# Grouped square roots, three score banks on each side and single-bank score units in a streamed attention kernel

## The chip, the cores and the metric

The kernel runs on one core of a Trainium2 chip. The metric is the device time of one execution in microseconds (us). TensorE (PE) multiplies matrices into PSUM, which has eight banks of 128 x 512 f32; VectorE (DVE), ScalarE (ACT) and GpSimd (POOL) work elementwise; SyncE (SP) issues most DMAs. Each engine runs its own instructions in order and waits for the others by semaphores.

## The reference

The input x is 8 sequences of 512 tokens of 128 channels, in f32. Eight layers follow, each x = x + f(layernorm(x)):

```python
x = x + L0_attn_a(ln(x))   # causal attention, 16 heads of 8 channels
x = x + L0_ffn(ln(x))      # sqrt((x @ cos A)^2 + (x @ sin A)^2)
x = x + L0_attn_b(ln(x))   # full attention with RoPE, 16 heads of 8
x = x + L0_ffn(ln(x))
x = x + L1_attn_a(ln(x))   # linear attention, then a GELU MLP inside
x = x + L1_ffn(ln(x))      # fp4-quantised gated MLP
x = x + L1_attn_b(ln(x))   # one head: softmax over the query axis of q k^T / 128
x = x + L1_ffn(ln(x))
```

The modulus in L0_ffn is the square root that the change groups.

## The kernel before, in words

The residual x stays in SBUF for the whole kernel as the tile X, four tiles of 128 tokens for each sequence. The six programs run one after the other with a barrier between: STREAM (`attention_stream`), linear attention, GELU MLP, fp4 MLP, `query_softmax`, fp4 MLP.

**The stream** computes the first four lines of the reference. It has 16 items (n = 0 to 15): items 0 to 7 are the eight sequences in layer a (causal), items 8 to 15 the same sequences in layer b (full). The heads of an item are worked on in four quads of four heads. `stream_order` writes down a time, in quads, for every piece of work; the list is sorted by it, and each engine walks the list in that order and does its own share. Nothing is reordered while it runs. For one quad:

- "first": the first score pass. PE writes q k^T, queries on partitions, into one of two PSUM banks (FIRST, L589). DVE takes the row maximum, with the mask added in layer a (L752), without in layer b (L757). The maxima are negated, turned (L597), copied by ACT (L476) and sent by DMA into the stacked queries.
- "scores": the second pass, two quads later (LAG). PE writes the scores, keys on partitions and the maximum already subtracted (L613), into one of two pairs of banks (SECOND). ACT takes the exponential of a unit into one of four `probs` tiles of 128 x 1024 (L500). A unit is two heads of 512 queries in layer b (8 units a quad); in layer a it is two heads or four, with the masked part left out (6 units a quad). In layer a POOL clears the half of the diagonal block that lies in the future (L380).
- "sum": PE multiplies the values with `probs` for one tile of keys, four heads side by side (L630), when the last unit of these keys is ready. ACT copies the sums (L508), PE turns them (L540), DVE divides.

PSUM is thus split as FIRST 0-1, SECOND 2-5, SUMS 6, MISC 7. MISC is used by turns for projections (L566, L570, L575), transposes, the turned maxima and the L0_ffn products.

After the last quad of an item comes its L0_ffn: layer norm, two products with cos and sin (L661), squares on ACT (L527), their sum on POOL (L391, `m_sum`), the square root on ACT (L531, `lengths`), the addition to x on POOL (L399, `m_add`). The square root needs another activation table than the exponential, so a table load stands before L531 and one before the next L500. There is one such square root for each item. The scratch of this part (m_xn, m_total and others) lies in X1, which the stream does not use otherwise.

**`query_softmax`** is a software pipeline over eight sequences with four stages, MEASURE, PROJECT, SCORE and SUM. `run_steps` emits steps with all engines' share; with four stages steps 4 to 7 form a hardware loop of two passes. In each step DVE does, in this order: normalise for PROJECT (L845), statistics for MEASURE, row maxima for SCORE (L1414), the value bias (L1421), the scaling of values (L1428), and the addition of SUM's result to X (L1433).

Of the kernel before, what the change touches and what calls it, by code (L numbers as in the profile page):

```python
# [84 lines left out]
LAG = 2  # L85


def score_units(causal):

    if not causal:  # L90
        first = [(qt, (j,), 512, 512) for qt in range(4) for j in range(4)]
        second = [(kt, pair, 512, 512) for kt in range(4) for pair in ((0, 1), (2, 3))]
        return first, second
    first = [(0, (0, 1, 2, 3), 128, 128), (1, (0, 1), 256, 256), (1, (2, 3), 256, 256)]
    first += [(qt, (j,), (qt + 1) * 128, 512) for qt in (2, 3) for j in range(4)]
    second = [(kt, pair, (4 - kt) * 128, 512) for kt in (0, 1) for pair in ((0, 1), (2, 3))]
    second += [(2, (0, 1, 2, 3), 256, 256), (3, (0, 1, 2, 3), 128, 128)]
    return first, second


def stream_order(seqs, late_loads):
# [9 lines left out]
    for n in range(2 * seqs):  # L111
        if n < seqs:
            f_at = [u / 11 for u in range(11)]
            s_at = [0.04, 0.20, 0.36, 0.50, 0.66, 0.82]
            sum_at = [0.50, 0.78, 1.03, 1.17]
            copy_at, tail_at = 1.19, 1.50
        else:
            f_at = [u / 16 for u in range(16)]
            s_at = [(i + 0.20) / 8 for i in range(8)]
            sum_at = [(kt + 1.45) / 4 for kt in range(4)]  # L120
            copy_at, tail_at = 1.20, 1.44
# [51 lines left out]
        at(r + 2.25, "mroot", n)  # L173
        at(r + 2.65, "madd", n)
# [5 lines left out]
def attention_stream(core, seqs, w, layers):  # L180
# [6 lines left out]
    def layer(n):  # L187
        return n // seqs
# [35 lines left out]
    probs = [sb(f"probs{i}", [P, 1024]) for i in range(4)]  # L224
# [10 lines left out]
    m_xn, m_total = spare[:, 0:4], spare[:, 4:8]  # L235
    m_xT = spare[:, 8:12].rearrange("p a c -> p (a c)")
    m_squares = [spare[:, 12 + 4 * i:16 + 4 * i].rearrange("p a c -> p (a c)").rearrange("p (t c) -> p t c", t=2)
                 for i in range(2)]
    angle, turns = [spare[:, 20 + 2 * i:22 + 2 * i].rearrange("p a c -> p (a c)") for i in range(2)]
# [7 lines left out]
    FIRST, SECOND, SUMS, MISC = 0, 2, 6, 7  # L247
# [78 lines left out]
    def gpsimd(g):  # L326
# [46 lines left out]
        def clear_future(n, q, gq, i):  # L373
            if not causal[layer(n)]:
                return
            _, heads, width, stride = second_of(n)[i]
            u = seconds(gq) + i
            diagonal = probs[u % 4][:].rearrange("p (h c) -> p h c", c=stride)[:, 0:len(heads), 0:P]
# [8 lines left out]
        def m_sum(n, q, gq, i):  # L387

            g.wait_ge(misc_free, uses_of_misc("mpart", n, 0, 1))
            for half in range(2):  # L390
                last = g.tensor_tensor(m_total[:, 2 * half:2 * half + 2], m_squares[half][:, :, 0:P],  # L391
                                       m_squares[half][:, :, P:2 * P], ALU.add)
            last.then_inc(m_total_ready, 1)

        def m_add(n, q, gq, i):
            b = n % seqs
            xs = X[:, 4 * b:4 * b + 4, :]
            g.wait_ge(m_length_ready, n + 1)
            g.tensor_tensor(xs, xs, m_total, ALU.add).then_inc(m_added, 1)  # L399
# [41 lines left out]
    def scalar(act):  # L441
# [48 lines left out]
        def exponentials(n, q, gq, i):  # L490

            _, heads, width, stride = second_of(n)[i]
            u = seconds(gq) + i
            b = u % 2
            src = ps[:, SECOND + 2 * b:SECOND + 2 * b + 2, :].rearrange("p a c -> p (a c)")
            v = lambda t: t.rearrange("p (h c) -> p h c", c=stride)[:, 0:len(heads), 0:width]
            act.wait_ge(scores_ready, u + 1)
            if u >= 4:
                act.wait_ge(sums_ready, freed_by(u - 4))
            act.activation(v(probs[u % 4][:]), v(src), ACT.Exp, scale=layers[layer(n)]["scale"])\  # L500
                .then_inc(scores_free, 1)
# [35 lines left out]
    def tensor(pe):  # L537
# [40 lines left out]
        def first_scores(n, q, gq, u):  # L578

            qt, heads, width, stride = first_of(n)[u]  # L580
            U = firsts(gq) + u
            if q % 2 == 0 and u == 0:

                pe.wait_ge(stack_loaded[q // 2], 16 * STACK_DMAS * (n + 1))
            if U >= 2:
                pe.wait_ge(max_free, U - 1)
            for o, j in enumerate(heads):
                h = 4 * q + j
                last = pe.matmul(ps[:, FIRST + U % 2, o * stride:o * stride + width],  # L589
                                 QS[n % 2][0:SHIFT_AT, h, qt * P:(qt + 1) * P], KS[n % 2][0:SHIFT_AT, h, 0:width],  # L590
                                 start=True, stop=True)
            last.then_inc(max_ready, 1)
# [7 lines left out]
        def scores(n, q, gq, i):  # L600
# [7 lines left out]
            if u >= 2:  # L608
                pe.wait_ge(scores_free, u - 1)
            for o, j in enumerate(heads):  # L610
                h = 4 * q + j
                bank, c = SECOND + 2 * (u % 2) + o * stride // 512, o * stride % 512
                last = pe.matmul(ps[:, bank, c:c + width], KS[n % 2][:, h, kt * P:(kt + 1) * P],  # L613
                                 QS[n % 2][:, h, 512 - width:512], start=True, stop=True)
            last.then_inc(scores_ready, 1)

        def sum_keys(n, q, gq, kt):
# [8 lines left out]
            for u, (at, heads, width, stride) in enumerate(second_of(n)):  # L626
                if at != kt:
                    continue
                for o, j in enumerate(heads):
                    last = pe.matmul(ps[32 * j:32 * j + DH + 1, SUMS, 512 - width:512], V[n % 2][:, kt, 4 * q + j, :],  # L630
                                     probs[(seconds(gq) + u) % 4][:, o * stride:o * stride + width],
# [37 lines left out]
    def vector(v):  # L669
# [71 lines left out]
        def maxima(n, q, gq, u):  # L741
            qt, heads, width, stride = first_of(n)[u]
            U = firsts(gq) + u
            src = ps[:, FIRST + U % 2, :].rearrange("p (h c) -> p h c", c=stride)[:, 0:len(heads), 0:width]
# [558 lines left out]
def query_softmax(core, items, w):  # L1303
# [25 lines left out]
    MEASURE, PROJECT, SCORE, SUM = range(4)  # L1329

    def gpsimd(g):
        def step(s, par, on):
            if on(MEASURE):
                root(g, s, par)
        run_steps(g, items, 4, step, before=1)


    def scalar(act):
# [19 lines left out]
        run_steps(act, items, 4, step, before=1)  # L1358

    def tensor(pe):  # L1360
# [37 lines left out]
        run_steps(pe, items, 4, step, before=1)  # L1398

    def vector(v):  # L1400
        v.sem_inc(out_free, 2)

        def step(s, par, on):
            if on(PROJECT):
                n, p = s - PROJECT, (par - PROJECT) % 2
                wait(v, misc_full, 4 * (n - 1) + 1)
                apply(v, n, xn[p], tiles(X, n, per), p).then_inc(xn_ready, 1)
            if on(MEASURE):
                measure(v, tiles(X, s, per), par)
# [24 lines left out]
        run_steps(v, items, 4, step, before=1)  # L1434
# [611 lines left out]
```

## Time and profile before

| | us |
|---|---|
| runs of the kernel | 2019.5, 2023.92 (median), 2027.14 |
| the profiled execution, its own time | 2022.12 |
| its span in the trace | 2020.4 |
| of that the stream | about 993 |
| of that `query_softmax` | 1755 to 1872 |

| engine | busy us (share of the span) |
|---|---|
| PE | 1686.0 (83%) |
| DVE | 1410.2 (70%) |
| ACT | 1056.4 (52%) |
| POOL | 520.4 (26%) |

The granted TensorE clock is a share of full speed. A busy PE is not a PE at its peak: the ends of matmuls are modelled, and the end of one overlaps the next.

### The profile page before, as it was taken

The numbers are of one execution on the slowest core, as the hardware profiler recorded it, in microseconds if no ns is written. First come the engines' busy times: TensorE is split into PE (matmuls) and PEld (weight loads), VectorE is DVE, ScalarE is ACT, GpSimd is POOL, SyncE is SP. The second block draws the span as 40 slices with busy tenths as digits, with TensorE's granted clock in tenths as the row PEclk, the third lists the DMA queues.
The fourth block names the chain that finished last, engine by engine and source line by source line (L and its number), as shares of the span: only waits on it lengthen the run. The fifth ranks groups of instructions, "written<-read, shape, count | busy, mean of one in ns | idle before, by whom it ended". The sixth has DMA issues, their size and how long they took to land. (4 is left out here: it accounts for less than half of the span.)

```text
span 2020.4 us, 36743 instructions
## 1 busy us (share of the span) xinstructions
PE 1686.0 (83%) x12704; PEld 941.8 (47%) x12781; DVE 1410.2 (70%) x4005; ACT 1056.4 (52%) x1727; POOL 520.4 (26%) x579
## 2 busy tenths in 40 slices
PE   3788888888988989888699999999997866688566
PEld 1233333333333333232366767767675645445454
DVE  6677777788777877775266667766674588655787
ACT  1466666656666666666354544445442355333453
POOL 5455555553333223300100000000002422200222
PEclk9799999999999999999699999999998988789798
DMA  5434332222221122200000000000000000000000
GB/s 95 58 62 96 61 65 49 49 47 46 48 48 24 25 48 48 40 9 1 0 1 2 2 2 2 2 3 1 2 2 1 1 0 0 1 0 0 6 16 21
DMA packets 56691, 49.82 MB, mean 25 GB/s; under 512 B 9221, under 2 KB 54469, under 8 KB 56517
## 3 DMA queue, kind: packets, MB, share of 16 engines
q1 hardware_dynamic: 53692, 46.45, 12.2%
q10 hardware_dynamic: 2824, 1.11, 0.4%
q8 instruction: 102, 1.67, 0.4%
q14 instruction: 73, 0.59, 0.1%
HBM read 7.10 MB, written 2.10 MB: 5 GB/s over the span
## 5 line engine op out<-in xcount | busy, mean ns | idle before, releaser
L500 ACT ACTIVATE at_probs<-ps 128x1024 f32<-128x1024 f32 (+1 forms) x448 | 427.6, 962 | 279.7 <-PE ps L613 273.7
L757 DVE TENSOR_REDUCE at_M<-ps 128x1 f32<-128x512 f32 x512 | 336.7, 686 | 109.5 <-PE ps L589 108.7
L589 PE MATMUL ps<-at_KS,at_QS 96*128 96x512 bf16 (+3 forms) x1024 | 321.8, 352 | 53.5 <-DVE at_M L752 21.0
L752 DVE CUSTOM_DVE_ANT_0 at_masked<-ps,at_mask_row 128x384 bf16<-128x384 f32 (+3 forms) x512 | 228.9, 486 | 74.9 <-PE ps L589 72.8
L630 PE MATMUL ps<-at_probs,at_V 128*9 128x512 f32 (+3 forms) x2048 | 233.0, 527 | 27.1 <-ACT at_C L508 12.3
L613 PE MATMUL ps<-at_QS,at_KS 128*128 128x512 bf16 x947 | 242.9, 343 | 15.1 <-DMA at_QS<-at_nmT 7.5
L589 PEld LDWEIGHTS ps<-at_KS,at_QS 96*128 96x128 bf16 x1024 | 91.6, 98 | 334.6 <-DVE at_M L757 150.7
L380 POOL TENSOR_SCALAR_AFFINE_SELECT at_probs<-at_probs 128x256 f32<-128x256 f32 (+1 forms) x192 | 93.9, 492 | 179.8 <-ACT at_probs L500 178.9
L613 PEld LDWEIGHTS ps<-at_QS,at_KS 128*128 128x128 bf16 x1024 | 93.2, 99 | 83.1 <-issue 25.2
L839 POOL TENSOR_TENSOR la_rstd<-la_vare,mhalf 128x4 f32<-128x4 f32 x16 | 16.1, 1008 | 414.7 <-DVE la_vare L834 414.7
L1250 DVE SCALAR_TENSOR_TENSOR la_phiq<-ps,la_ezq 128x512 f32<-128x512 f32 x64 | 44.2, 690 | 111.8 <-ACT la_ezq L1101 111.8
L1579 POOL TENSOR_TENSOR fp_rounded<-fp_level,fp_scale 128x960 f32<-128x960 f32 (+2 forms) x36 | 59.1, 1641 | 188.8 <-DVE fp_level L1734 188.8
L1678 PE MATMUL ps<-gate_up,fp_xT 128*128 128x352 f32 x256 | 104.0, 559 | 2.5 <-ACT fp_xT L1602 2.5
L1195 PE MATMUL ps<-la_V,la_S 128*64 128x65 f32 x2048 | 103.0, 221 | 0.2 <-issue 0.2
L1259 DVE TENSOR_TENSOR la_S<-ps,keep_kq 128x512 f32<-128x512 f32 x128 | 82.4, 685 | 27.0 <-PE ps L1167 26.1
L1088 ACT ACTIVATE la_V<-ps 128x512 f32<-128x512 f32 x64 | 38.2, 597 | 111.3 <-PE ps L1141 111.3
L1095 ACT ACTIVATE la_belowq<-ps 128x512 f32<-128x512 f32 x64 | 38.2, 597 | 110.8 <-PE ps L1148 110.8
L1660 PE MATMUL ps<-ident,fp_rounded 128*128 128x128 f32 x64 | 15.0, 319 | 92.8 <-POOL fp_rounded L1579 92.8
L1195 PEld LDWEIGHTS ps<-la_V,la_S 128*64 128x64 f32 x2048 | 91.7, 137 | 0.4 <-issue 0.4
L630 PEld LDWEIGHTS ps<-at_probs,at_V 128*9 128x9 f32 x2048 | 31.1, 88 | 103.8 <-issue 40.8
L1191 PE MATMUL ps<-la_state,la_phiq 128*64 128x130 f32 x768 | 75.5, 275 | 0.0
L1678 PEld LDWEIGHTS ps<-gate_up,fp_xT 128*128 128x128 f32 x256 | 57.3, 235 | 36.8 <-issue 18.0
(258 smaller groups left out, 3373.7 us busy)
## 6 DMA issues: line engine op xcount, KB each, us to landing
at_QS<-at_splitq SPq DMA_DIRECT2D x288, 64.0 KB
at_KS<-at_splitk SPq DMA_DIRECT2D x279, 64.0 KB
out<-X SPq DMA_DIRECT2D x8, 256.0 KB, 2.3
at_QS<-at_nmT ACTq DMA_DIRECT2D x64, 8.0 KB
at_KS<-at_splitk ACTq DMA_DIRECT2D x9, 64.0 KB
w_raw<-fp_weights SPq DMA_DIRECT2D x1, 560.0 KB, 5.7
w_wv<-L_attn_a_wv SPq DMA_DIRECT2D x1, 512.0 KB, 6.8
w_wo<-L_attn_a_wo SPq DMA_DIRECT2D x1, 512.0 KB, 6.6
```

The costliest lines, as they stand in the source:

```text
L380: g.affine_select(out=diagonal, in_=diagonal, compare_op=ALU.is_ge, fill=0.0, base=0, pattern=[[0, len(heads)], [1, P]], channel_multiplie ...
L500: act.activation(v(probs[u % 4][:]), v(src), ACT.Exp, scale=layers[layer(n)]["scale"])\
L589: last = pe.matmul(ps[:, FIRST + U % 2, o * stride:o * stride + width], QS[n % 2][0:SHIFT_AT, h, qt * P:(qt + 1) * P], KS[n % 2][0:SHIFT_A ...
L613: last = pe.matmul(ps[:, bank, c:c + width], KS[n % 2][:, h, kt * P:(kt + 1) * P], QS[n % 2][:, h, 512 - width:512], start=True, stop=True)
L630: last = pe.matmul(ps[32 * j:32 * j + DH + 1, SUMS, 512 - width:512], V[n % 2][:, kt, 4 * q + j, :], probs[(seconds(gq) + u) % 4][:, o * s ...
L752: last = v.tensor_tensor_reduce(masked[U % 4][:, o * stride:o * stride + width], src[:, o, :], mask_row[:, 512 - width:512], 1.0, 4 * NEG, ...
L757: v.tensor_reduce(M[gq % 2][:, heads[0]:heads[-1] + 1, qt], src, AX.X, ALU.max).then_inc(max_free, 1)
L1191: pe.matmul(outs[rows, c, 0:2 * AUG], phi[0][j % 4][:, c * P:(c + 1) * P][:, rows], state[j % 2][:, c - 1, :], start=True, stop=False)
L1195: last = pe.matmul(outs[rows, c, AUG * a:AUG * (a + 1)], S[a][j % 2][:, c * P:(c + 1) * P][:, rows], V[par][:, c, 2 * j + a, :], start=c = ...
L1259: v.tensor_tensor(S[a][j % 2][:].rearrange("p (c q) -> p c q", c=4), ps[:, SCORES + a, :].rearrange("p (c q) -> p c q", c=4), over(core["k ...
L1579: g.tensor_tensor(in_blocks(rounded[par][:, lo:hi]), in_blocks(level[par][:, lo:hi]), over(scale[par][:, lo // BLOCK:hi // BLOCK], 2, BLOC ...
L1678: last = pe.matmul(ps[:, GATE_UP + 2 * t + i, 0:INNER], xT[p][:, t * P:(t + 1) * P], gate_up[:, i, :], start=True, stop=True)
```

## The change

- A second-pass unit is now at most 512 columns, one bank: one head in layer b (16 units a quad), one head, two of 256 or four of 128 in layer a (11 units a quad). The times of the units in the order are new; those of the sums are not.
- FIRST and SECOND have three banks each. The waits for a free bank look back three units instead of two. `probs` becomes eight tiles of 128 x 512, the same space.
- The square root waits until up to four items have their sums of squares: items 0-3, 4-7, 8-11, 12-14 and 15. m_total has four parts; one `activation` covers those of a group, and the additions to x follow 0.4 quads apart.
- In `query_softmax` the addition to X becomes a fifth stage, ADD, one step later, between the normalising and the statistics. With five stages `run_steps` emits no hardware loop for eight items: all steps are written out.

```diff
+ROOTS = 4
+def root_group(n, items):
+    first = n - n % ROOTS
+    last = min(first + ROOTS, items) - 1
+    if last == items - 1:
+        return (n, n) if n == last else (first, last - 1)
+    return first, last
...
-        second = [(kt, pair, 512, 512) for kt in range(4) for pair in ((0, 1), (2, 3))]
+        second = [(kt, (j,), 512, 512) for kt in range(4) for j in range(4)]
...
-    second = [(kt, pair, (4 - kt) * 128, 512) for kt in (0, 1) for pair in ((0, 1), (2, 3))]
-    second += [(2, (0, 1, 2, 3), 256, 256), (3, (0, 1, 2, 3), 128, 128)]
+    second = [(kt, (j,), (4 - kt) * 128, 512) for kt in (0, 1) for j in range(4)]
+    second += [(2, (0, 1), 256, 256), (2, (2, 3), 256, 256), (3, (0, 1, 2, 3), 128, 128)]
...
-            s_at = [0.04, 0.20, 0.36, 0.50, 0.66, 0.82]
+            s_at = [0.03, 0.11, 0.19, 0.27, 0.35, 0.43, 0.50, 0.57, 0.66, 0.74, 0.83]
...
-            s_at = [(i + 0.20) / 8 for i in range(8)]
+            s_at = [(i + 0.20) / 16 for i in range(16)]
...
-        at(r + 2.25, "mroot", n)
-        at(r + 2.65, "madd", n)
+        lo, hi = root_group(n, 2 * seqs)
+        if n == hi:
+            at(r + 2.25, "mroot", n)
+            for i in range(hi - lo + 1):
+                at(r + 2.65 + 0.4 * i, "madd", lo + i)
...
-    probs = [sb(f"probs{i}", [P, 1024]) for i in range(4)]
+    probs = [sb(f"probs{i}", [P, 512]) for i in range(8)]
...
-    FIRST, SECOND, SUMS, MISC = 0, 2, 6, 7
+    FIRST, SECOND, SUMS, MISC = 0, 3, 6, 7
...
-            act.wait_ge(m_total_ready, n + 1)
-            act.activation(m_total, m_total, ACT.Sqrt).then_inc(m_length_ready, 1)
+            lo, hi = root_group(n, items)
+            act.wait_ge(m_total_ready, hi + 1)
+            some = spare[:, 16 + 4 * (lo % ROOTS):20 + 4 * (hi % ROOTS)]
+            act.activation(some, some, ACT.Sqrt).then_inc(m_length_ready, hi - lo + 1)
...
-            if U >= 2:
-                pe.wait_ge(max_free, U - 1)
+            if U >= 3:
+                pe.wait_ge(max_free, U - 2)
...
-            if u >= 2:
-                pe.wait_ge(scores_free, u - 1)
+            if u >= 3:
+                pe.wait_ge(scores_free, u - 2)
...
-    MEASURE, PROJECT, SCORE, SUM = range(4)
+    MEASURE, PROJECT, SCORE, SUM, ADD = range(5)
...
+            if on(ADD):
+                n, p = s - ADD, (par - ADD) % 2
+                xs = tiles(X, n, per)
+                v.wait_ge(out_ready, n + 1)
+                v.tensor_tensor(flat(xs), flat(xs), ps[:, OUT + p, :], ALU.add).then_inc(out_free, 1)
             if on(MEASURE):
...
-            if on(SUM):
-                n, p = s - SUM, (par - SUM) % 2
-                xs = tiles(X, n, per)
-                v.wait_ge(out_ready, n + 1)
-                v.tensor_tensor(flat(xs), flat(xs), ps[:, OUT + p, :], ALU.add).then_inc(out_free, 1)
```

## Rows read from the trace of the kernel before

**Rows 1.** Busy time by engine in the stretches of layers a, b and `query_softmax`.

```profile
core 0: us, PE busy (x) PEld busy (x) DVE busy (x) ACT busy (x) POOL busy (x), PEclk, DMA share, GB/s
90.00:435.00 345.00, 292.00 (x2179) 134.31 (x2206) 266.11 (x1189) 215.40 (x299) 189.05 (x269) 0.98 0.33 63
435.00:945.00 510.00, 455.94 (x2474) 160.43 (x2521) 387.33 (x832) 334.42 (x404) 144.74 (x141) 0.98 0.18 34
...
1755.00:1872.00 117.00, 93.80 (x448) 61.21 (x448) 63.11 (x200) 39.04 (x89) 8.06 (x8) 0.89 0.00 1
```

**Rows 2.** The same for one sequence of layer b, quad by quad.

```profile
690.52:709.01 18.49, 15.35 (x82) 5.39 (x81) 13.16 (x25) 13.57 (x17) 10.66 (x11) 1.00 0.04 10
709.01:724.29 15.28, 14.50 (x69) 4.16 (x71) 9.88 (x19) 9.28 (x12) 6.79 (x6) 0.89 0.49 84
724.29:739.80 15.51, 14.74 (x89) 5.98 (x88) 11.95 (x25) 9.91 (x14) 0.00 (x0) 1.00 0.29 61
739.80:755.07 15.27, 13.68 (x75) 4.87 (x77) 13.84 (x40) 9.70 (x14) 2.03 (x2) 1.00 0.01 2
```

**Rows 3.** Waits in total: who waited for whom, us, times, longest us.

```profile
ACT at_probs L500 <- PE ps L613: 273.7, 308, 8.5
...
PEld ps L589 <- DVE at_M L757: 150.7, 262, 1.1
...
PEld ps L589 <- DVE at_M L752: 72.0, 127, 1.3
...
PEld ps L630 <- ACT at_probs L500: 36.1, 68, 4.2
...
PEld ps L570 <- ACT at_nmT L476: 26.3, 14, 2.3
...
PEld ps L630 <- POOL at_probs L380: 22.7, 38, 2.6
```

**Rows 4.** Order of time, ACT and PE around a square root of layer b.

```profile
702.17 1.93 ACT L500 ACTIVATE at_probs<-ps 128x1024 f32<-128x1024 f32 x2
...
704.70 1.28 ACT L531 ACT_TABLE_LOAD   x1
...
706.64 1.28 ACT L500 ACT_TABLE_LOAD   x1
...
708.86 0.25 ACT L476 ACTIVATE at_nmT<-ps 32x128 bf16<-32x128 bf16 x1
...
709.16 1.19 PE L570 MATMUL ps<-at_xT,w_b_wk 128*128 128x512 f32 x2 [2.02 <-ACT at_nmT L476]
```

**Rows 5.** Groups by shape in the first 1200 us: busy us, mean ns | idle before.

```profile
L500 ACT ACTIVATE at_probs<-ps 128x1024 f32<-128x1024 f32 x352 | 359.1, 1023 | 224.3 <-PE ps L613 218.3 <-remote 3.2
...
L380 POOL TENSOR_SCALAR_AFFINE_SELECT at_probs<-at_probs 128x256 f32<-128x256 f32 x128 | 52.3, 412 | 117.5 <-ACT at_probs L500 116.7
...
L380 POOL TENSOR_SCALAR_AFFINE_SELECT at_probs<-at_probs 128x512 f32<-128x512 f32 x64 | 41.7, 651 | 62.4 <-ACT at_probs L500 62.2
...
L500 ACT ACTIVATE at_probs<-ps 128x512 f32<-128x512 f32 x32 | 19.1, 597 | 39.3 <-PE ps L613 39.3
...
L531 ACT ACTIVATE X<-X 128x512 f32<-128x512 f32 x16 | 10.1, 629 | 0.4 <-POOL X L391 0.2
```

**Rows 6.** Order of time, PE at a first-pass matmul of layer b.

```profile
744.98 0.60 PE L613 MATMUL ps<-at_QS,at_KS 128*128 128x512 bf16 x2
745.56 0.39 PE L589 MATMUL ps<-at_KS,at_QS 96*128 96x512 bf16 x1
746.41 0.39 PE L589 MATMUL ps<-at_KS,at_QS 96*128 96x512 bf16 x1 [0.46 <-DVE at_M L757]
```

**Rows 7.** Order of time, DVE and PE between two steps of `query_softmax`.

```profile
1806.29 0.69 DVE L1428 TENSOR_TENSOR qs_vs<-qs_val,qs_inverse 128x512 f32<-128x512 f32 x1
1807.43 0.69 DVE L1433 TENSOR_TENSOR X<-X,ps 128x512 f32 x1 [0.45 <-PE ps L1395]
1808.04 1.11 DVE L845 TENSOR_SCALAR qs_xn<-X,qs_meanvar,qs_rstd 128x128 f32 x4
...
1809.28 0.65 PE L1367 MATMUL ps<-ident,qs_xn 128*128 128x128 f32 x4 [2.03 <-DVE qs_xn L845]
```

More of the change, by code:

```diff
@@ L234, in attention_stream @@
     spare = core["X1"]
-    m_xn, m_total = spare[:, 0:4], spare[:, 4:8]
-    m_xT = spare[:, 8:12].rearrange("p a c -> p (a c)")
-    m_squares = [spare[:, 12 + 4 * i:16 + 4 * i].rearrange("p a c -> p (a c)").rearrange("p (t c) -> p t c", t=2)
+    m_xn = spare[:, 0:4]
+    m_xT = spare[:, 4:8].rearrange("p a c -> p (a c)")
+    m_squares = [spare[:, 8 + 4 * i:12 + 4 * i].rearrange("p a c -> p (a c)").rearrange("p (t c) -> p t c", t=2)
                  for i in range(2)]
-    angle, turns = [spare[:, 20 + 2 * i:22 + 2 * i].rearrange("p a c -> p (a c)") for i in range(2)]
+    m_total = [spare[:, 16 + 4 * i:20 + 4 * i] for i in range(ROOTS)]
+    angle, turns = [spare[:, 28 + 2 * i:30 + 2 * i].rearrange("p a c -> p (a c)") for i in range(2)]
     m_stats = sb("m_stats", [P, 4, 6])
@@ L389, in m_sum @@
             g.wait_ge(misc_free, uses_of_misc("mpart", n, 0, 1))
+            if n == ROOTS - 1:
+                g.wait_ge(waves_ready, 1)
             for half in range(2):
-                last = g.tensor_tensor(m_total[:, 2 * half:2 * half + 2], m_squares[half][:, :, 0:P],
+                last = g.tensor_tensor(m_total[n % ROOTS][:, 2 * half:2 * half + 2], m_squares[half][:, :, 0:P],
                                        m_squares[half][:, :, P:2 * P], ALU.add)
@@ L493, in exponentials @@
             u = seconds(gq) + i
-            b = u % 2
-            src = ps[:, SECOND + 2 * b:SECOND + 2 * b + 2, :].rearrange("p a c -> p (a c)")
+            src = ps[:, SECOND + u % 3, :]
             v = lambda t: t.rearrange("p (h c) -> p h c", c=stride)[:, 0:len(heads), 0:width]
             act.wait_ge(scores_ready, u + 1)
-            if u >= 4:
-                act.wait_ge(sums_ready, freed_by(u - 4))
-            act.activation(v(probs[u % 4][:]), v(src), ACT.Exp, scale=layers[layer(n)]["scale"])\
+            if u >= 8:
+                act.wait_ge(sums_ready, freed_by(u - 8))
+            act.activation(v(probs[u % 8][:]), v(src), ACT.Exp, scale=layers[layer(n)]["scale"])\
                 .then_inc(scores_free, 1)
@@ L607, in scores @@
                     pe.wait_ge(signs_loaded, 16 * 2)
-            if u >= 2:
-                pe.wait_ge(scores_free, u - 1)
+            if u >= 3:
+                pe.wait_ge(scores_free, u - 2)
             for o, j in enumerate(heads):
                 h = 4 * q + j
-                bank, c = SECOND + 2 * (u % 2) + o * stride // 512, o * stride % 512
-                last = pe.matmul(ps[:, bank, c:c + width], KS[n % 2][:, h, kt * P:(kt + 1) * P],
+                c = o * stride
+                last = pe.matmul(ps[:, SECOND + u % 3, c:c + width], KS[n % 2][:, h, kt * P:(kt + 1) * P],
                                  QS[n % 2][:, h, 512 - width:512], start=True, stop=True)
@@ L1334, in step @@
                 root(g, s, par)
-        run_steps(g, items, 4, step, before=1)
+        run_steps(g, items, 5, step, before=1)
     def scalar(act):
@@ L1357, in step @@
                                    scale=SCALE, accum_out=total[p][:, t:t + 1]).then_inc(E_ready, 1)
-        run_steps(act, items, 4, step, before=1)
+        run_steps(act, items, 5, step, before=1)
     def tensor(pe):
@@ L1397, in step @@
                 last.then_inc(out_ready, 1)
-        run_steps(pe, items, 4, step, before=1)
+        run_steps(pe, items, 5, step, before=1)
     def vector(v):
@@ L1428, in step @@
                 v.tensor_tensor(vs[p][:], val[p][:], over(inverse[p][:], 2, P), ALU.mult).then_inc(vs_ready, 1)
-            if on(SUM):
-                n, p = s - SUM, (par - SUM) % 2
-                xs = tiles(X, n, per)
-                v.wait_ge(out_ready, n + 1)
-                v.tensor_tensor(flat(xs), flat(xs), ps[:, OUT + p, :], ALU.add).then_inc(out_free, 1)
-        run_steps(v, items, 4, step, before=1)
+        run_steps(v, items, 5, step, before=1)
     return dict(gpsimd=gpsimd, scalar=scalar, tensor=tensor, vector=vector)
```

12 lines of the change are left out of this document (6 added, 6 removed).

## The prediction, made before the changed kernel was run

> **What bounds the kernel now.** I first read busy time by stretch. In the stream no engine is full: PE is busy 292 of 345 us in layer a and 456 of 510 in layer b, DVE 266 and 387, ACT 215 and 334 [rows 1]. The PE figure is flattered. In [rows 6] a first-pass matmul starts 0.58 us after a pair that needs 0.43 (two at about 0.215, the pace at which such matmuls follow each other: the pair's 0.60 us is two paces plus a tail of 0.17), and the next one 0.85 us later, so 0.63 us is empty where the row books 0.46. So I take it that PE, DVE and ACT hold each other up: each walks a fixed order, and a late engine stops the others because only two banks lie between them.
>
> Then one sequence of layer b, quad by quad [rows 2]. It takes 64.55 us. The quads look alike but for the first, 18.49 us against 15.3 to 15.5, and the second has a granted clock of 0.89, which is 0.11 x 15.28 = 1.7 us lost at half speed. The last quad has DVE busy 13.84 of 15.27 us: there DVE is nearly the bound. In the second it is busy only 9.88.
>
> The waits say what stops PE [rows 3]. The weight loads of the first pass waited for DVE for 150.7 + 72.0 = 222.7 us over 389 times, 0.57 us each. The k projection waited for ACT's copy of the turned maxima for 26.3 us, 14 times in 16 items, 1.88 us each. Sums waited for ACT 36.1 us and for POOL's mask 22.7 us. ACT waited for PE 273.7 us: as a whole it has room. The order of time around a square root [rows 4] explains the k projection: ACT loads a table at 704.70, takes the root, loads the other table at 706.64, goes on with exponentials at 707.92, and reaches the copy at 708.86, for which PE has stood 2.02 us at L570.
>
> **Square roots.** Each costs ACT 1.28 + 0.63 + 1.28 = 3.2 us in one piece [rows 4, 5]. Of 16 single ones, 11 go (items 0-2, 4-6, 8-10, 12, 13). What a block costs in time is not 3.2 us but what PE waits behind it: 1.88 us on average, 2.02 in the row shown, and in some cases part of the 1.7 us of low clock that follows the wait. I take 2.2 us: 11 x 2.2 = 24 us gained. The blocks kept grow: per 512 elements an exponential costs 1023 - 597 = 426 ns more [rows 5], so a root over four items takes 3 x 0.43 = 1.3 us more and over three 0.85. Three of four, one of three: 3 x 1.3 + 0.85 = 4.7 us, fully on the path since PE waits there already; I take 4. Net -20. Bounds: +5 (ACT is late anyway) and -45 (all 3.2 us and some clock). What is late next is the k projection's own chain, copy of the maxima, which then waits for an exponential or two only. The additions on POOL keep their number, 16; four now follow a root 0.4 quads, some 6 us, apart. No DMA is added or moved, and SP's waits for stacks look at the same events. The last item keeps its own root, so the end of the stream is as before.
>
> The Trainium skill (ScalarE: Activation LUTs, "What ACT_TABLE_LOAD costs") puts a switch at 2.66 us, load and drain together. The trace shows 1.28 us from load to next work, so the measurement decides; by the page 22 fewer switches would be 58 us of ACT, by the row 28.
>
> **Three banks for the first pass.** The most that can be won is the true emptiness behind the 389 waits. Of the mean 0.57 us a part is still filled by the pair streaming since the last load: 0.43 less one load of 0.10 is 0.33, so 0.24 us is empty, 389 x 0.24 = 93 us. A third bank lets PE be one more maximum, some 0.62 us of DVE work, ahead. It helps where DVE was held by something passing (the wait for a layer norm's root, a block of four small operations), and not where DVE is full, as in the last quad of [rows 2]. I take a little over a third: -35. Bounds 0 and -93.
>
> **Single-bank units.** Exponentials: layer a 6 to 11 a quad, layer b 8 to 16, over 32 quads each: 448 become 864, 416 more. Two in a row of 1024 take 1.93 us where each lasts 1.02 [rows 4], so 0.11 us of an operation hides under the next one. If ACT is always supplied, an extra instruction costs (0.597 - 0.11) x 2 - (1.023 - 0.11) = 0.06 us, if each is met alone 2 x 0.597 - 1.023 = 0.17 us: 25 to 71 us more of ACT. It has 273.7 us of waits for PE to put them in, so mostly nothing. What is lost is elasticity: PE may lead ACT by two units of 0.91 us before and by three of 0.49 us now, 1.8 against 1.5 us, and the sums stand closer behind their last unit (in layer b 0.16 quads after it instead of 0.21, 2.5 us instead of 3.2). POOL's masks: 6 selects become 11. By 412 and 651 ns for 256 and 512 columns [rows 5] one of 128 is about 0.29 us, so a quad has 8 x 0.29 + 2 x 0.41 + 0.65 = 3.8 us instead of 4 x 0.41 + 2 x 0.65 = 2.9; POOL is busy 189 of 345 us in layer a [rows 1], with operations of up to 1.28 us in which a mask is queued, and sums behind it. Against this a unit is free sooner for PE. I take +12 us for the whole. Bounds -5 and +71.
>
> The Trainium skill (same page and section) gives an ACTIVATE a fixed 186 ns beside 0.833 ns an element, 93 ns of which hide under the one before. This speaks against the split. By it the 416 cost at least 39 us of ACT, an estimate between the two ends above; the rows agree in the slope (426 ns for 512).
>
> **`query_softmax`.** Between two steps [rows 7] DVE ends the scaling at 1806.98, waits for PE's sum, adds from 1807.43, and normalises only from 1808.04; PE starts the next transposes at 1809.28 after an idle 2.03 us. With the addition behind the normalising, the latter can start at about 1807.0, 1.0 us earlier, and then DVE's chain over ACT's last exponential sets the pace. The addition then delays the statistics and with them the first row maximum, by about 0.5 us, but the exponentials wait for the projection copies on ACT, later than the maxima. Five such steps have a normalising after an addition: -5. Written-out steps I put at nothing: the loop's seam shows no gap to remove. A higher clock (0.89 here [rows 1]) adds perhaps 1: -6 in all. Bounds -2 and -12.
>
> **Sum.** 2022.1 - 20 - 35 + 12 - 6 = 1973 us, on the profiled execution's own time. The median of the runs is 1.8 us above that: 1975 us.
>
> **Rivals.**
>
> - DVE is the bound and a third bank changes nothing. For it: DVE busy 13.84 of 15.27 us in one quad. Against: 9.9 to 13.2 in the other three. 2022 - 20 + 12 - 6 = 2008. Chance 0.22.
> - The three engines come apart well. Roots -30, first pass -60, units +5, `query_softmax` -9: 1928. For it: even with the tails counted PE books 58.3 of the 64.55 us of [rows 2], so without waits a sequence of layer b could shrink by 6 us and more, eight of them by 50. Against: half of what is empty is at other waits (MISC, sums). Chance 0.20.
> - ACT's splitting lands on the path: slower. If the exponentials are met one at a time and each quad's sums wait for them, all 71 us count: 2022 - 20 - 35 + 71 - 6 = 2032; it needs 61 of the 71 us on PE's path to decide against the kernel, and with the first-pass gain gone, 26. For it: sums already waited 36.1 us for ACT. Against: 273.7 us of room. Chance 0.10, of which 0.07 ends above 2034.
> - Masks late: in layer a POOL's extra 0.9 us a quad all in front of sums, +29 instead of a few: 1995. It lies in the forecast's neighbourhood and is counted there.
>
> The forecast (1950 to 2000) has 0.48.
>
> **Numbers.** The range is 1930 to 2016: it leaves out the upper part of the third rival and part of the second. A measurement can tell about 0.5%, 10 us. Faster than 2014: 0.84; within: 0.09; slower than 2034: 0.07. Within the likeliest case alone 1950 to 2000.
>
> **What would show it.** The 18.5 us quads of layer b become about 16 except after grouped roots, with waits of L570 for the copy near 0 in 11 items; two table loads per group, 10 in place of 32. The waits of L589 for DVE fall by a third or more. Exponentials of 512 last 0.60 us each and ACT's busy time changes by the 25 to 71 us above less some 30 for loads and roots. Sums' waits for POOL and ACT rise somewhat. Transposes L1367 wait about 1 us in place of 2. The prediction is wrong if PE's waits only change their names: second-pass matmuls waiting for ACT, or DVE at over 90% in all quads.

## The result and the profile after

The changed kernel takes 1952.63 us in the median of four runs (1949.83 to 1954.47), against 2022.47 before: 0.9651 of it, 95% interval [0.9628, 0.9675], 70 us less. (2022.47 is the median of four runs of the kernel before; the 2023.92 above was that of three.) The range given, 1930 to 2016, held it; the forecast was 1975. The profiled execution took 1949.83 us.

The page of the changed kernel, its span and the busy time by engine:

```profile
span 1948.0 us, 37580 instructions
...
PE 1659.1 (85%) x12701; PEld 945.7 (49%) x12781; DVE 1400.6 (72%) x4005; ACT 1046.9 (54%) x2110; POOL 543.9 (28%) x739
```

PE's work is the same, yet it books 27 us less. Part of that is the clock: the mean granted clock of the stream rises from 0.96 to 0.97, and the share missing to full speed times the time is 40 us before and 28 now, some 12 us less (an estimate from rounded rows). The rest may lie in the modelled ends of matmuls, which overlap more where matmuls follow each other closely; that isn't shown. The barrier behind the stream falls at about 930 us instead of 993, 63 of the 72 us by which the spans differ; `query_softmax` gives 11.7, and the other programs together take about 2 us more.

Busy time by engine of the changed kernel, quad by quad in one sequence of layer b without a root, then the stretch of `query_softmax` from its first transposes to its last sum, in the kernel before and in the changed one; columns as in [rows 1] and [rows 2] (the stretch in [rows 1] is a wider one):

```profile
592.20:608.00 15.80, 14.49 (x79) 5.34 (x80) 11.40 (x24) 10.63 (x23) 8.31 (x9) 1.00 0.01 2
608.00:620.86 12.86, 12.80 (x72) 4.14 (x71) 10.64 (x21) 9.66 (x21) 7.91 (x7) 1.00 0.48 80
620.86:635.59 14.73, 14.17 (x89) 6.12 (x89) 11.71 (x25) 10.07 (x21) 0.00 (x0) 1.00 0.43 93
635.59:649.99 14.40, 13.54 (x77) 4.91 (x78) 14.04 (x41) 10.28 (x21) 2.03 (x2) 1.00 0.00 1
```

```profile
1759.06:1871.23 112.17, 93.80 (x448) 61.17 (x448) 59.74 (x186) 39.04 (x89) 7.05 (x7) 0.90 0.00 1
```

```profile
1697.60:1798.10 100.50, 88.32 (x448) 59.14 (x448) 58.24 (x187) 39.00 (x89) 7.05 (x7) 0.94 0.00 1
```

Against [rows 2] the sequence takes 57.79 us instead of 64.55. The first quad falls from 18.49 to 15.80, the second from 15.28 to 12.86 and shows the full clock, 1.00 for 0.89. In the last quad DVE is busy 14.04 of 14.40 us, so it is close to being the bound there. What each part of the change gave in these quads stands with the experiments.

Waits of the changed kernel in total, those of [rows 3] (L606 is the first pass, L630 the second, L647 the sums, L587 the k projection):

```profile
ACT at_probs L515 <- PE ps L630: 162.8, 221, 5.1
...
PEld ps L606 <- DVE at_M L774: 105.8, 174, 0.9
...
PEld ps L647 <- ACT at_probs L515: 56.1, 109, 1.5
...
PEld ps L606 <- DVE at_M L769: 50.9, 81, 1.1
...
PEld ps L647 <- POOL at_probs L394: 38.4, 66, 3.9
...
PEld ps L630 <- ACT at_probs L515: 30.6, 48, 4.1
...
PEld ps L587 <- ACT at_nmT L492: 11.6, 11, 5.5
```

The first pass waits for DVE 255 times and 156.7 us instead of 389 and 222.7. The sums wait more, 94.5 us for 58.8. The second pass waits for ACT (30.6 us; before it was 5.0). The k projection waits 11.6 us for 26.3, but its longest wait has grown from 2.3 to 5.5 us: that is a grouped root.

Timeline of the changed kernel around a grouped root in layer b on ACT (start, duration, and then the work):

```profile
721.68 1.28 ACT L548 ACT_TABLE_LOAD   x1
722.97 1.91 ACT L548 ACTIVATE X<-X 128x2048 f32<-128x2048 f32 x1
724.90 1.28 ACT L515 ACT_TABLE_LOAD   x1
...
727.17 0.25 ACT L492 ACTIVATE at_nmT<-ps 32x128 bf16<-32x128 bf16 x1
```

The same stretch on PE, then PE behind the grouped root of layer a; in brackets the wait and what ended it:

```profile
726.85 0.61 PE L630 MATMUL ps<-at_QS,at_KS 128*128 128x512 bf16 x1 [3.04 <-ACT at_probs L515]
...
727.68 1.92 PE L587 MATMUL ps<-at_xT,w_b_wk 128*128 128x512 f32 x2
```

```profile
283.80 2.07 PE L587 MATMUL ps<-at_xT,w_a_wk 128*128 128x512 f32 x2 [5.05 <-ACT at_nmT L492]
```

The block is 4.5 us, as forecast (1.28 + 1.91 + 1.28). In layer b PE first stands at the second pass, where it may lead ACT by three units only. In layer a the copy of the maxima starts 1.5 us after the block has ended (283.49 for 282.03), behind exponentials and the copy of the sums, and PE stands 5.05 us. Both times the projection behind it runs at a low clock: the granted clock is 0.50, the lower level, during the 1.92 us in layer b, and 0.54 in the 6 us from 283.80 on in layer a. In [rows 4] the same pair took 1.19 us.

**One measure for all stream kernels.** ACT copies the sums once a quad, so the distance from one copy (at_C, L508 before, L523 in the changed kernel) to the fourth after it is the time of a sequence. Sequences of the same kind mostly agree within 0.3 us in one kernel, so this resolves what whole runs can't. The exception in the table is units_alone in layer a, from 51.6 to 52.6. The last two columns are the first sequence, and the fourteen behind it taken together.

| us per sequence | a, no root | a, root | b, no root | b, root | the first | the next fourteen |
|---|---|---|---|---|---|---|
| before | | 49.7 | | 64.6 | 46.3 | 807.2 |
| only_roots (grouped) | 45.5 | 55.1 | 60.8 | 67.0 | 43.8 | 779.2 |
| units_alone (single roots) | | 51.6 to 52.6 | | 64.9 | 44.3 | 829.0 |
| first_two_banks (grouped) | 46.7 | 55.4 | 61.5 | 66.4 | 49.6 | 787.5 |
| first_two_second_four (grouped) | 46.7 | 55.3 | 61.5 | 66.3 | 46.6 | 786.4 |
| single_roots | | 50.9 | | 61.4 | 48.1 | 796.2 |
| changed kernel (grouped) | 45.3 | 55.0 | 57.8 | 62.5 | 42.5 | 750.1 |

The first sequence is not a matter of the edits alone: old_qs and qs_written_out below have the changed kernel's stream to the letter, and theirs takes 47.8 and 41.4 us where the changed kernel's takes 42.5. Their next fourteen take 752.0 and 752.2 us. So some 6 us of a difference between whole runs can be an accident of the start.

### The profile page after: what moved, and what is told of

Its sections match the earlier page's. It is cut to its first block and busy times, and to the rows that moved or that the text cites. A ratio compares the mean times of both kernels' runs of the same rounds, so it can differ in the third digit from the quotient of the medians.

```text
span 1948.0 us, 37580 instructions
## 1 busy us (share of the span) xinstructions
PE 1659.1 (85%) x12701; PEld 945.7 (49%) x12781; DVE 1400.6 (72%) x4005; ACT 1046.9 (54%) x2110; POOL 543.9 (28%) x739
## 5 line engine op out<-in xcount | busy, mean ns | idle before, releaser
L515 ACT ACTIVATE at_probs<-ps 128x512 f32<-128x512 f32 (+1 forms) x864 | 458.7, 581 | 219.7 <-PE ps L630 162.8
L774 DVE TENSOR_REDUCE at_M<-ps 128x1 f32<-128x512 f32 x512 | 330.1, 682 | 78.7 <-PE ps L606 77.5
L606 PE MATMUL ps<-at_KS,at_QS 96*128 96x512 bf16 (+3 forms) x1024 | 324.2, 348 | 39.9 <-DMA at_KS<-at_splitk 18.2
L630 PE MATMUL ps<-at_QS,at_KS 128*128 128x512 bf16 x944 | 294.0, 342 | 10.7 <-ACT at_probs L515 10.5
L647 PE MATMUL ps<-at_probs,at_V 128*9 128x512 f32 (+3 forms) x2048 | 228.7, 519 | 26.2 <-POOL at_probs L394 19.2
L606 PEld LDWEIGHTS ps<-at_KS,at_QS 96*128 96x128 bf16 x1024 | 94.4, 99 | 253.0 <-DVE at_M L774 105.8
L394 POOL TENSOR_SCALAR_AFFINE_SELECT at_probs<-at_probs 128x128 f32<-128x128 f32 (+2 forms) x352 | 118.1, 346 | 125.2 <-ACT at_probs L515 119.7
L630 PEld LDWEIGHTS ps<-at_QS,at_KS 128*128 128x128 bf16 x1024 | 97.7, 99 | 101.9 <-ACT at_probs L515 30.6
L647 PEld LDWEIGHTS ps<-at_probs,at_V 128*9 128x9 f32 x2048 | 30.4, 88 | 115.1 <-ACT at_probs L515 56.1
```

The costliest lines, as they stand in the source:

```text
L515: act.activation(v(probs[u % 8][:]), v(src), ACT.Exp, scale=layers[layer(n)]["scale"])\
L606: last = pe.matmul(ps[:, FIRST + U % 3, o * stride:o * stride + width], QS[n % 2][0:SHIFT_AT, h, qt * P:(qt + 1) * P], KS[n % 2][0:SHIFT_A ...
L630: last = pe.matmul(ps[:, SECOND + u % 3, c:c + width], KS[n % 2][:, h, kt * P:(kt + 1) * P], QS[n % 2][:, h, 512 - width:512], start=True, ...
L774: v.tensor_reduce(M[gq % 2][:, heads[0]:heads[-1] + 1, qt], src, AX.X, ALU.max).then_inc(max_free, 1)
```

## The experiments

**The roots: single_roots and only_roots.** The first is the changed kernel with

```diff
-ROOTS = 4
+ROOTS = 1
```

the second the kernel before with `root_group`, four parts of m_total and the grouped `lengths`, and nothing else.

> The changed kernel with one square root for each item again (16 roots instead of 5). By the prediction's price (2.2 us for each root that goes, 4 us back for the longer ones) it takes 20 us more than the changed kernel, 1973 us. Rival: with the new banks PE still leads ACT by only 1.5 us, so a block of 3.2 us on ACT lands on PE's path nearly whole; then 11 x 3.2 less 4.7 is 30 us more and with the clock after each wait up to 38: 1983 to 1991 us. In the trace the first case has PE idle about 2 us at each root, the second 3 us or more.

> The kernel before with the grouped roots alone. By the prediction 20 us less than before, 2002 us; by the rival (the block counts whole) 30 to 38 less, 1984 to 1992. If the root's worth is the same here and in the changed kernel, the parts add up; if it is smaller here, the old two banks hid part of it.

Measured: single_roots 1997.07 us, 0.9877 of before [0.9861, 0.9894], 44 us above the changed kernel. only_roots 1987.86 us, 0.9837 [0.9821, 0.9854], 33 us below before. The price of 2.2 us for a root falls. The table gives its true size: a single root costs 4.2 us (a) and 3.8 (b) in the kernel before (49.7 - 45.5, 64.6 - 60.8), and 5.6 and 3.6 in the changed one. A grouped one costs 4.7 in layer b (62.5 - 57.8) and 9.7 in layer a (55.0 - 45.3). The block is not hidden, and in layer a more than the block is lost. Part of the 9.7 belongs to the place: the one grouped root of layer a falls into the fifth sequence, and with single roots that sequence takes 52.1 us where its neighbours take 50.9 to 51.2. Like for like the grouped root costs 2.9 us more than the single one (55.0 - 52.1), of which 1.3 is its length.

The trace of single_roots shows what comes on top of the block. Its k projection behind a root of layer a, its sequence in layer a, and the same sequence of the changed kernel; then the first two quads of its sequence in layer b:

```profile
201.56 2.08 PE L587 MATMUL ps<-at_xT,w_a_wk 128*128 128x512 f32 x2 [3.78 <-ACT at_nmT L492]
```

```profile
184.93:235.83 50.90, 42.41 (x315) 20.10 (x316) 37.54 (x170) 32.33 (x64) 29.71 (x58) 0.93 0.40 97
```

```profile
174.41:219.75 45.34, 40.09 (x315) 19.20 (x316) 37.45 (x170) 29.01 (x61) 28.49 (x57) 1.00 0.48 109
```

```profile
629.34:647.60 18.26, 15.19 (x81) 5.37 (x81) 12.43 (x25) 13.80 (x25) 10.69 (x11) 0.99 0.04 11
647.60:661.54 13.94, 13.88 (x70) 4.27 (x70) 9.72 (x19) 9.67 (x20) 6.75 (x6) 0.89 0.47 77
```

In layer a PE stands 3.78 us at the k projection, which then runs at a granted clock of 0.50, and the sequence has 0.93 where the changed kernel has 1.00. In layer b the root takes 2.5 us in the first quad (18.26 for 15.80) and 1.1 in the second (13.94 for 12.86), the one with the clock of 0.89.

**The third bank of the first pass: first_two_banks.**

```diff
-            if U >= 3:
-                pe.wait_ge(max_free, U - 2)
+            if U >= 2:
+                pe.wait_ge(max_free, U - 1)
...
-                last = pe.matmul(ps[:, FIRST + U % 3, o * stride:o * stride + width],
+                last = pe.matmul(ps[:, FIRST + U % 2, o * stride:o * stride + width],
```

and the same bank number in `maxima`.

> The changed kernel with two banks for the first pass (the third lies idle). By the prediction the third bank is worth 35 us: 1988 us. Rival: it is worth nothing, DVE being the bound, and the gain in the stream came from the single-bank units: 1952 to 1957 us. A worth between 15 and 50 goes with the prediction.

Measured: 1993.75 us, 0.9868 [0.9851, 0.9884], 41 us above the changed kernel. A sequence without a root is 1.4 us longer in layer a and 3.7 in layer b. The fourteen sequences behind the first are 37 us longer, so most of the 41 is the bank, but 7 us of the distance between the two profiled executions lie in the first sequence, which can be an accident. The waits of its weight loads are somewhat above those of before, 248.3 us for 222.7:

```profile
PEld ps L606 <- DVE at_M L774: 168.2, 280, 1.4
...
PEld ps L606 <- DVE at_M L769: 80.1, 142, 1.1
```

The third bank is what shortened them. Where it helped is told by the quads of a sequence of layer b with two banks, to be set beside those of the changed kernel above:

```profile
619.06:635.31 16.25, 14.81 (x79) 5.16 (x80) 11.37 (x23) 10.83 (x22) 8.31 (x9) 1.00 0.01 2
635.31:649.32 14.01, 13.60 (x72) 3.72 (x71) 10.71 (x21) 10.01 (x20) 7.92 (x7) 1.00 0.42 89
649.32:665.01 15.69, 15.06 (x89) 5.75 (x89) 11.82 (x25) 10.41 (x21) 0.00 (x0) 1.00 0.30 73
665.01:680.59 15.58, 14.18 (x77) 4.50 (x78) 14.32 (x41) 10.58 (x21) 2.02 (x2) 1.00 0.00 1
```

The bank gives 0.45, 1.15, 0.96 and 1.18 us in the four quads. The most comes in the last one, where DVE was busy 14.32 of 15.58 us and the prediction expected nothing.

**A fourth bank for the second pass: first_two_second_four.**

```diff
-    FIRST, SECOND, SUMS, MISC = 0, 3, 6, 7
+    FIRST, SECOND, SUMS, MISC = 0, 2, 6, 7
...
-            if u >= 3:
-                pe.wait_ge(scores_free, u - 2)
+            if u >= 4:
+                pe.wait_ge(scores_free, u - 3)
```

with two first-pass banks, as above.

> The changed kernel with its third first-pass bank given to the second pass: two first, four second. The run with two and three took 1994 us. If PE's short lead over ACT (three units) is what the split costs, a fourth unit gives back 10 to 25 us: 1969 to 1984, though not the 1953 of the changed kernel. Rival: the second pass has banks enough and only the number of operations costs: 1990 to 1996 us.

Measured: 1991.43 us, 0.9858 [0.9818, 0.9898]; first_two_banks had 1993.75. The sequences without a root are the same to 0.1 us, those with one to 0.5. The second pass waits less for ACT, 17.3 us for 27.3, and it gains no time. The rival holds: with two first-pass banks a lead of four units instead of three is worth nothing. So the shorter lead of PE over ACT, which the prediction named as a loss of the single-bank units, shows no cost here.

**The units by themselves: units_alone.** The changed kernel with all three edits undone: `ROOTS = 1`, two first-pass banks, the old `query_softmax`.

> The changed kernel with two banks for the first pass, single roots and the old query_softmax: what is left of the change is the single-bank units, three of them, the eight probs tiles and the new times. The prediction put them at +12 us over before, bounds -5 and +71, which gives 2034 us. If the parts measured so far add up (44 for the roots, 41 for the third first-pass bank, 13 for query_softmax, 98 in sum, where the whole is 70), the units cost 28: 2050 us. If the roots' price depends on the other parts, the result lies nearer to 2030.

Measured: 2042.11 us, 1.0101 of before [1.0063, 1.0139]: longer by 13 to 28 us, 21 in the middle. Its sequences of layer b are 0.3 us longer than before, those of layer a 1.9 to 2.9. In sequences without a root (first_two_banks against only_roots) the units cost 0.7 us in layer b and 1.2 in layer a. There are 256 more exponentials in layer b and 160 in layer a, and layer b loses less. So the longer list of ACT's operations is hardly the main cost; no run tests it by itself.

**The masks: masks_paired.** In layer a one POOL operation clears two neighbouring one-head units; `probs` is one tensor of eight parts for it.

```diff
+            if len(heads) == 1 and i % 2 == 0:
+                return
...
+            if len(heads) == 1 and u % 8:
+                blocks = [(all_probs[:, u % 8 - 1:u % 8 + 1, 0:P], 2, 2)]
```

> The changed kernel with the masks of two neighbouring one-head units of layer a in one POOL operation (7 or 8 a quad instead of 11). The units alone had made a sequence of layer a 2.5 us longer (52.2 against 49.7) and one of layer b only 0.3 (64.9 against 64.6). If that comes from POOL's extra masks, a sequence of layer a shrinks by 1 to 2.5 us: 1934 to 1946 us in all. Rival: it comes from ACT's shorter operations and the sums' shorter distance: 1950 to 1956 us, and layer a stays at 45.3.

Measured: 1949.43 us, 0.9669 [0.9642, 0.9697], not to be told from the changed kernel's 0.9651. POOL's masks fall from 352 to 208 operations:

```profile
L394 POOL TENSOR_SCALAR_AFFINE_SELECT at_probs<-at_probs 128x128 f32<-128x128 f32 x256 | 72.5, 294 | 94.0 <-ACT at_probs L515 90.7 <-DVE at_xn L719 0.9
```

```profile
L404 POOL TENSOR_SCALAR_AFFINE_SELECT at_probs<-at_probs 128x256 f32<-128x256 f32 x176 | 71.7, 409 | 93.0 <-ACT at_probs L525 89.6
```

The first row is of the changed kernel, the second of this one; 128 columns take 294 ns, the 0.29 us estimated. A sequence of layer a stays at 45.2 to 45.6 us: that the number of masks is what the units cost there is not borne out. The test isn't a pure one, since the first unit of a pair now waits for the mask until the second is ready.

**Later sums: sums_later.**

```diff
-            sum_at = [0.50, 0.78, 1.03, 1.17]
+            sum_at = [0.57, 0.85, 1.10, 1.18]
...
-            sum_at = [(kt + 1.45) / 4 for kt in range(4)]
+            sum_at = [(kt + 1.65) / 4 for kt in range(4)]
```

> The changed kernel with each sum as far behind its last unit as before the change (layer b 0.21 quads instead of 0.16, layer a 0.30 instead of 0.23). If the prediction's loss of elasticity lies at the sums, their waits for ACT and POOL (94 us of weight-load waits) fall by half and the time by 5 to 15 us: 1938 to 1948 us. Rival: the sums only pass on how late ACT is, and PE then waits at the next second-pass unit: 1950 to 1956 us.

Measured: 1947.24 us, 0.9620 [0.9582, 0.9659]: by whole runs at the edge of what can be told. By sequences it is plain: 56.6 us instead of 57.8 in layer b, 45.7 to 45.8 instead of 45.3 to 45.4 in layer a. In layer b the shorter distance of the sums cost 1.2 us a sequence, more than the 0.7 that the units cost there; in layer a it cost nothing. The rival was half right: the sums' waits fall from 94.5 to 53.0 us, those of the second pass for ACT rise from 30.6 to 52.6 and those of the first pass for DVE from 156.7 to 171.5, yet time is won. The last quad of a sequence of layer b shows that DVE was not yet its bound in the changed kernel, since it now takes 14.02 us instead of 14.40:

```profile
640.30:654.32 14.02, 13.65 (x77) 4.90 (x78) 13.45 (x40) 10.13 (x21) 2.02 (x2) 1.00 0.00 1
```

**query_softmax: old_qs and qs_written_out.** The first has the old function whole. The second has five stages, and so no hardware loop, but the addition at the end of the step:

```diff
-            if on(ADD):
-                n, p = s - ADD, (par - ADD) % 2
+            if on(SUM):
+                n, p = s - SUM, (par - SUM) % 2
```

moved behind the scaling of the values.

> The changed kernel with query_softmax as it was before (addition at the end of the step, four stages, hardware loop). The prediction had 6 us for it: 1959 us. The two traces differ by 11.7 us from the stage's first transposes to its last matmul (112.2 and 100.5 us), of which the clock is a part; by that the run takes 1964 us, and its stage shows 112 us again.

> The changed kernel with the addition of query_softmax back at the end of the step, but still five stages without a hardware loop. If all of the 12 to 13 us come from the place of the addition, the stage takes 112 us and the run 1965, as with the old one. If the loop itself cost something, it lies between 1953 and 1965.

Measured: old_qs 1965.70 us, 0.9725 [0.9709, 0.9741], 13 above the changed kernel; qs_written_out 1959.28, 0.9687 [0.9651, 0.9723], about half way. The stage in the two, by engine as above:

```profile
1708.80:1820.20 111.40, 93.01 (x448) 61.43 (x448) 59.76 (x186) 39.04 (x89) 7.05 (x7) 0.90 0.00 1
```

```profile
1703.00:1808.60 105.60, 88.16 (x448) 59.20 (x448) 59.36 (x186) 39.00 (x89) 7.05 (x7) 0.94 0.00 1
```

The starts of PE's transposes show why. First with the loop (old_qs), then written out (qs_written_out), then the changed kernel, three steps each:

```profile
1744.21 0.96 PE L1384 MATMUL ps<-ident,qs_xn 128*128 128x128 f32 x4 [1.88 <-DVE qs_xn L862]
1758.40 0.66 PE L1384 MATMUL ps<-ident,qs_xn 128*128 128x128 f32 x4 [2.03 <-DVE qs_xn L862]
1771.00 0.65 PE L1384 MATMUL ps<-ident,qs_xn 128*128 128x128 f32 x4 [2.14 <-DVE qs_xn L862]
```

```profile
1738.38 0.66 PE L1384 MATMUL ps<-ident,qs_xn 128*128 128x128 f32 x4 [1.81 <-DVE qs_xn L862]
1750.71 0.66 PE L1384 MATMUL ps<-ident,qs_xn 128*128 128x128 f32 x4 [1.81 <-DVE qs_xn L862]
1763.04 0.66 PE L1384 MATMUL ps<-ident,qs_xn 128*128 128x128 f32 x4 [1.81 <-DVE qs_xn L862]
```

```profile
1731.84 0.66 PE L1384 MATMUL ps<-ident,qs_xn 128*128 128x128 f32 x4 [0.75 <-DVE qs_xn L862]
1743.11 0.66 PE L1384 MATMUL ps<-ident,qs_xn 128*128 128x128 f32 x4 [0.75 <-DVE qs_xn L862]
1754.38 0.66 PE L1384 MATMUL ps<-ident,qs_xn 128*128 128x128 f32 x4 [0.74 <-DVE qs_xn L862]
```

With the loop a step takes 14.19, then 12.60 us; written out 12.33 and 12.33; with the addition moved 11.27 and 11.27. The four steps of old_qs from 1744.21 on, with their granted clock:

```profile
1744.21:1758.40 14.19, 12.15 (x57) 7.97 (x57) 7.91 (x27) 4.65 (x11) 1.01 (x1) 0.88 0.01 2
1758.40:1771.00 12.60, 10.46 (x57) 7.13 (x57) 7.89 (x27) 4.65 (x11) 1.01 (x1) 1.00 0.00 0
1771.00:1785.18 14.18, 12.15 (x56) 7.70 (x57) 7.95 (x27) 4.65 (x11) 1.01 (x1) 0.88 0.00 0
1785.18:1799.24 14.06, 12.14 (x56) 7.97 (x57) 7.73 (x25) 4.65 (x11) 1.01 (x1) 0.88 0.00 0
```

At full clock (1.00) the step with the loop is 0.27 us longer than the written-out one, in PE's idle time (1.88 to 2.14 us for 1.81). Three of the four steps fall to 0.88, some 1.5 us each; the written-out steps of both other kernels stay at 1.00. Of the 5.8 us between the stages of old_qs and qs_written_out (111.40 and 105.60) the clock is thus the larger part. That the loop brings the low clock about rests on one trace of each kernel. The addition's place is worth 1.06 us a step, as forecast.

**A later root, and the three together: root_later, combined, two_shifts.**

```diff
-            at(r + 2.25, "mroot", n)
+            at(r + 2.54, "mroot", n)
...
-                at(r + 2.65 + 0.4 * i, "madd", lo + i)
+                at(r + 2.94 + 0.4 * i, "madd", lo + i)
```

combined adds sums_later and masks_paired, two_shifts sums_later alone.

> The changed kernel with the grouped root 0.29 quads later in the order, behind the copy of the maxima, the copy of the sums and the k projection instead of in front of them. In the changed kernel a sequence with a grouped root takes 9.7 us more than its neighbours in layer a (55.0 against 45.3) and 4.7 more in layer b (62.5 against 57.8); in layer a PE stands 5.05 us at the k projection. If this place in the order is part of the price, the difference falls to 5 us or less in layer a and 3 to 4 in layer b: 5 to 9 us in all, 1944 to 1948. Rival: the block of 4.5 us counts wherever it lies, since PE can lead ACT by three units only: 1951 to 1955.

> The changed kernel with the later roots, the later sums and the paired masks together. The later sums alone gave 1947 us. If root and masks keep their worth and all three add, 1925 to 1940 us; if each only moves the same wait, 1943 to 1950.

> The changed kernel with the later roots and the later sums, without the paired masks. All three together took 1933 us, the later sums alone 1947, and 10 of these 14 us lie in the first four quads, where the profile of the later sums shows 51.6 us and that of the combination 41.7, with the same sequences behind. If the start-up is an accident of when the first loads and the low clock fall, this kernel can land anywhere from 1933 to 1945 us, with its sequences of layer b at 56.6 us either way. If the paired masks are worth something at the start, it takes 1941 to 1945 with a slow start, as the later sums alone.

Measured: root_later 1948.72 us, 0.9668 [0.9640, 0.9695]; combined 1933.38, 0.9581 [0.9557, 0.9606]; two_shifts 1939.03, 0.9602 [0.9579, 0.9626]. In root_later the grouped root of layer a costs 6.3 us (51.6 - 45.3) instead of 9.7, those of layer b 5 to 6 instead of 4.7. The k projection is passed with 0.40 us of waiting, and PE stands at the next thing that needs ACT, the product that folds a bias:

```profile
280.87 1.13 PE L587 MATMUL ps<-at_xT,w_a_wk 128*128 128x512 f32 x2 [0.40 <-ACT at_nmT L492]
...
289.23 0.80 PE L569 MATMUL ps<-w_b_wo,at_bv_wide 128*128 128x128 f32 x2 [4.16 <-ACT at_bv_wide L461]
```

The rival holds in the main: the block counts wherever it lies, and what the later place wins in one sequence it loses in others. Over the fourteen sequences root_later takes 750.2 us and the changed kernel 750.1, and as whole runs the two can't be told apart. combined has the lowest time here; its sequences are close to those of sums_later (56.6 us in layer b, 45.1 to 45.6 in layer a). The layer a sequence with a root is back at 54.8 us, so what root_later gained there (51.6) was not repeated; two_shifts has it again (51.7). Of the 14 us that combined gains over sums_later 10 lie in the first four quads (41.7 against 51.6 us); two_shifts, 5.6 us above combined, has 48.2 there. This start takes 41.4 to 51.6 us over the kernels of this study, without an order that fits their edits. Behind the start the next fourteen sequences take 741.9 us in sums_later, 739.7 in combined and 737.1 in two_shifts: the pairing of the masks gains nothing there. So 9 us or so of combined's gain over the changed kernel, the later sums in layer b, is explained; the rest I don't claim for an edit.

## Why the prediction was right, and where its sizes were off

The sign and the range held, and the roots and the third bank are the two large terms, as forecast. Their sizes were off, and some of the errors cancel: the whole came out 70 us faster where 47 were forecast. By runs the parts are -44 (roots), -41 (bank), +21 (units), -13 (`query_softmax`): -77, where the whole is -70. They need not add up. The roots and the bank were each taken out of the changed kernel, the units were added to the kernel before, and the start blurs the sums: single_roots and first_two_banks have a first sequence 5.6 and 7.1 us longer than the changed kernel's. The fourteen sequences behind it are cleaner. There the units cost 21.8 us, the roots give 41.4 with two banks (units_alone against first_two_banks), and the third bank then gives 37.4: together the 57 us between 807.2 and 750.1. With three banks the roots give 46.1, so the two help each other by some 5 us.

- **Roots**: forecast -20, measured -44 in the changed kernel and -33 in the kernel before. The step that failed is "what a block costs in time is not 3.2 us but what PE waits behind it: 1.88 us". That row is one wait, the first that PE meets. Behind it the second pass waits for exponentials and the clock falls (0.93 over a sequence of layer a, 0.89 in the second quad of layer b): 3.6 to 5.6 us for a block of 3.2. The sums don't wait longer for single roots (88.5 us against 94.5). The kept roots were mis-sized as well: I added 1.3 us for their length, and in layer a one costs 9.7 us, 2.9 more than a single one at the same place.
- **Third bank**: forecast -35, measured -41 by runs and -37 by sequences. The size was right; that it is a little over a third of 93 us was a choice, and its coming out that near is partly luck. Where the gain lies was wrong: "not where DVE is full, as in the last quad of [rows 2]". With two banks DVE was busy 14.32 of 15.58 us there, and the third bank gave 1.18 us, more than in any other quad.
- **Single-bank units**: forecast +12, bounds -5 and +71, measured +21 [13 to 28]. The named mechanisms fared differently. A fourth bank did not help, fewer masks did not either, and the later sums gained 1.2 us a sequence in layer b. ACT's longer list was never tested by itself. What makes a sequence of layer a 1.2 us longer stays open.
- **query_softmax**: forecast -6, bounds -2 and -12, measured -13 by runs and 10.9 us by the stage (111.40 for 100.50). The moved addition gave its 1.06 us a step. The step that failed is "written-out steps I put at nothing: the loop's seam shows no gap to remove": 0.27 us a step was spread in PE's idle time, and the steps at the low clock were worth more than that.
- **Rivals**: that DVE is the bound and a third bank changes nothing is refuted (first_two_banks), even for the quad that spoke for it. That the engines come apart well (1928) went too far: the whole came to 1953, between the forecast and that rival, since the units cost their 21 us and a grouped root 4.7 to 9.7. ACT's split all on the path, +71 us: refuted in its size, since the units as a whole cost 21, and 256 more operations come with 0.7 us a sequence in layer b.

The Trainium skill (ScalarE: Activation LUTs, "What ACT_TABLE_LOAD costs") has a switch at 2.66 us with its drain, and 1.28 us is what lies between load and next work in this trace too. What a switch and back cost the kernel, though, 3.6 to 5.6 us with the root between them, could be read from neither: only the sequences without a root show it.

## What to carry to other kernels

A block on an engine that others follow closely can cost its whole length and more, however idle that engine is on average (here 3.6 to 5.6 us for 3.2): price it by the block, not by the first wait behind it, and look for what is next in line. A busy share of some 90% in a stretch does not mean that a deeper buffer is worth nothing there: the third bank gained the most in the last quad, where DVE was 92% busy with two banks and 97.5% with three. In a periodic kernel, measure the period: it resolves tenths of a microsecond where whole runs differ by five, and it keeps an accident of the start out of the comparison.

## What was not expected of the hardware

A hardware loop of two passes around four steps came with 0.27 us more a step in PE's idle time and no seam that stands out. Of the clock the rows show this. Written out, PE was idle 1.81 us before each of the steps shown, and all ran at the full clock (12.33 us a step, eight f32 matmuls in 3.60 us). In old_qs the idle times before its steps were 1.88, 2.03, 2.14 and 2.03 us, and the granted clock of the steps 0.88, 1.00, 0.88 and 0.88; the same 2.03 us stands before a step at full clock and before one that is not. What decides between them no run here shows. The first sequence of the stream takes from 41.4 to 51.6 us from kernel to kernel, and 41.4 to 47.8 in three kernels with the same stream. Its mean granted clock is 1.00 in the two shorter ones of these three (42.5 and 41.4 us) and 0.93 in the longer. Behind it, sequences of one kind mostly repeat to 0.3 us.
